# Taking the maximum of the value weights in four pieces, one per feed-forward step

## What is computed

```
x = x + 0.5 * ffn(layernorm(x))
x = x + attn(layernorm(x))
x = x + 0.5 * ffn(layernorm(x))

ffn:  h = x
      for blk in range(3):                    # three blocks
          y = qlora_linear(h, 2*blk)          # dequantised 128x128 weight, bias, low-rank term
          y = gelu(layernorm(y, g[blk], b[blk]))
          h = h + qlora_linear(y, 2*blk+1)
attn: xq, xk = x Q[h], x K[h]                 # 16 heads, rank 64
      attn = softmax(xq xk^T / sqrt(128))
      out  = sum over heads of attn x VO[h]   # VO: 16 x 128 x 128
```

## Time and profile before

| | |
|---|---|
| median of 3 runs | 987.42 us |
| profiled execution, its own time | 987.76 us |
| its span | 986.0 us |
| TensorE busy | 956.5 us (97%) |
| VectorE busy | 855.1 us (87%) |
| ScalarE busy | 807.4 us (82%) |
| GpSimd busy | 829.5 us (84%) |
| granted TensorE clock, mean | 0.997 |

### The profile page before, as it was taken

The page is one execution under the profiler, slowest core; times in us unless marked ns, Lnnn a source line. Parts: engine busy times, 40 slices in busy tenths (PEclk is TensorE's granted clock), DMA queues, the critical chain, the costliest instruction groups (busy, mean ns, idle before and its releaser), DMA issues.

```text
span 986.0 us, 19436 instructions
## 1 busy us (share of the span) xinstructions
PE 956.5 (97%) x6005; PEld 509.7 (52%) x6005; DVE 855.1 (87%) x1741; ACT 807.4 (82%) x1341; POOL 829.5 (84%) x938
## 2 busy tenths in 40 slices
PE   4889899999999999999999999999999999999998
PEld 4668344444444444444444444444444444444777
DVE  7678999999999999999999999999999988986664
ACT  4866788888888888888888888888888988888774
POOL 3645699899998999899999999999999998899552
PEclk9999999999999999999999999999999999999999
DMA  9000322222222222222222222222222222221002
GB/s 253 1 1 9 89 65 65 65 59 68 61 59 62 63 63 59 62 63 65 66 65 65 65 65 65 65 65 57 63 62 61 64 61 61 63 62 33 2 1 86
DMA packets 71744, 59.89 MB, mean 61 GB/s; under 512 B 11168, under 2 KB 70560, under 8 KB 71648
## 3 DMA queue, kind: packets, MB, share of 16 engines
q1 hardware_dynamic: 71392, 58.31, 24.0%
q10 hardware_dynamic: 256, 0.39, 0.2%
HBM read 6.23 MB, written 2.10 MB: 8 GB/s over the span
## 4 chain that ended last, share of the span: by engine, by line
PE 91%; DVE 5%; POOL 2%; issue 1%; DMA 1%; ACT 0%; SPq 0%; POOLq 0%; DVEq 0%; ACTq 0%
PE ps L1219 12%; PE ps L1211 11%; PE ps L1221 11%; PE ps L1220 11%; PE ps L1212 11%; PE ps L1204 7%; PE ps L1195 3%; PE ps L1238 3%; PE ps L1234 3%; PE ps L1235 3%; PE ps L1113 3%; PE ps L1196 3%; PE ps L1197 3%; PE ps L1142 2%; PE ps L1123 1%; PE ps L1154 1%
## 5 line engine op out<-in xcount | busy, mean ns | idle before, releaser
L470 POOL TENSOR_TENSOR p_lo<-work_b,p_hi 128x1024 f16<-128x1024 f32 x256 | 540.1, 2131 | 46.3 <-ACT p_hi L615 45.7
L920 DVE TENSOR_REDUCE mcol<-ps 128x2 f16<-128x1024 f32 x256 | 301.4, 1222 | 2.2 <-PE ps L1204 2.1
L610 ACT ACTIVATE work_b<-ps,exp_scale 128x1024 f32<-128x1024 f32 x256 | 271.5, 1111 | 36.5 <-PE ps L1212 36.3
L615 ACT ACTIVATE p_hi<-work_b 128x1024 f16<-128x1024 f32 x256 | 256.0, 1055 | 0.0
L1211 PE MATMUL ps<-head_ops 128*128 128x512 f16 x512 | 194.1, 379 | 2.9 <-DVE mcol L920 1.5
L1219 PE MATMUL ps<-p_hi,xn_hi 128*128 128x512 f16 x512 | 194.7, 380 | 0.9 <-POOL p_lo L470 0.9
L1220 PE MATMUL ps<-p_hi,xn_lo 128*128 128x512 f16 x512 | 194.0, 379 | 0.0
L1221 PE MATMUL ps<-p_lo,xn_hi 128*128 128x512 f16 x512 | 194.0, 379 | 0.0
L1212 PE MATMUL ps<-head_ops 128*128 128x512 f16 x512 | 194.0, 379 | 0.0
L479 POOL TENSOR_TENSOR x<-x,o_sb 128x512 f32<-128x512 f32 x126 | 160.2, 1271 | 5.4 <-POOL rstd L447 0.2
L931 DVE STREAM_TRANSPOSE head_ops<-mcol 32x128 f16<-32x128 f16 x512 | 155.4, 304 | 9.3
(11 more groups left out here) (139 smaller groups left out, 1378.9 us busy)
## 6 DMA issues: line engine op xcount, KB each, us to landing
head_ops<-pair_ops SPq DMA_DIRECT2D x512, 64.0 KB, 2.0
head_ops<-pair_ops SPq DMA_DIRECT2D x128, 128.0 KB, 2.4
x<-x_dram SPq DMA_DIRECT2D x8, 256.0 KB, 5.9
out<-x SPq DMA_DIRECT2D x8, 256.0 KB, 2.5
vo_last<-wvo_dram SPq DMA_DIRECT2D x1, 1024.0 KB, 11.9
qk<-wq_dram SPq DMA_DIRECT2D x1, 512.0 KB, 5.2
qk<-wk_dram SPq DMA_DIRECT2D x1, 512.0 KB, 6.0
scl<-scales_dram ACTq DMA_DIRECT2D x8, 48.0 KB, 5.3
```

The costliest lines, as they stand in the source:

```text
L470: pool.tensor_tensor(p_lo[:, k % 2, rows, :], p32[:, k % 2, rows, :], p_hi[:, k % 2, rows, :], ALU.subtract).then_inc(plo_done, 1)
L610: nc.scalar.activation(p32[:, k % 2, 2 * a:2 * a + 2, :], s_ps[a], ACT.Exp, scale=exp_scale[:, 0:1]).then_inc(exp_done, 1)
L615: nc.scalar.activation(p_hi[:, k % 2, 2 * a:2 * a + 2, :], p32[:, k % 2, 2 * a:2 * a + 2, :], ACT.Copy).then_inc(phi_done, 1)
L920: nc.vector.tensor_reduce(mcol[:, pair % 2, :, t, 0], max_ps[pair == 1][t % 2], AX.X, ALU.max, negate=True).then_inc(max_red, 1)
```

## The change

The reduce over the 2048 columns of the value weights is cut into four reduces of 512 columns (four heads). Their results go to a new tile `vo_amax` of four columns, and a fifth, small reduce takes the maximum of these four. Piece q waits for 2(q+1) folds where the one reduce waited for 8. The pieces are issued in steps 3, 3, 4 and 5 and the maxima of Q and K in steps 1 and 2 where they were in steps 2 and 3. Also the place within the step is another one: K's maximum and the first, third and fourth piece stand between `seed` and `z_scaled`, Q's maximum and the second piece behind `z_scaled`.

```
+        vo_amax = sb("vo_amax", [128, 4])
...
-                dve.wait_ge(vo_folded, H // 2)
-                link(dve, nc.vector.tensor_reduce(amax[:, 2:3], vo32[:, :, :].rearrange("p h d -> p (h d)"), AX.X,
-                                                  ALU.max, apply_absolute_value=True))
-                nc.vector.tensor_scalar(amax[:, 0:3], amax[:, 0:3], 1e-30, None, ALU.max).then_inc(prep_v, 1)
+                q = n - 2
+                heads = slice(q * H // 4, (q + 1) * H // 4)
+                dve.wait_ge(vo_folded, 2 * (q + 1))
+                link(dve, nc.vector.tensor_reduce(vo_amax[:, q:q + 1], vo32[:, heads, :].rearrange("p h d -> p (h d)"),
+                                                  AX.X, ALU.max, apply_absolute_value=True))
+                if q == 3:
+                    link(dve, nc.vector.tensor_reduce(amax[:, 2:3], vo_amax[:, :], AX.X, ALU.max))
+                    nc.vector.tensor_scalar(amax[:, 0:3], amax[:, 0:3], 1e-30, None, ALU.max).then_inc(prep_v, 1)
...
                 seed(0, i)
+                if i == 2:
+                    weight_maxima(1)
+                if i == 3:
+                    weight_maxima(2)
+                if i in (4, 5):
+                    weight_maxima(i)
                 if i >= 1:
                     z_scaled(0, i - 1)
-                if i in (2, 3):
-                    weight_maxima(i - 2)
-                if i == 5:
-                    weight_maxima(2)
+                if i == 1:
+                    weight_maxima(0)
+                if i == 3:
+                    weight_maxima(3)
```

## The result

| | before | after |
|---|---|---|
| median of the runs | 987.42 us (7 runs, 986.00 to 987.95) | 983.17 us (7 runs, 983.11 to 984.57) |
| profiled execution, its own time | 987.76 us | 983.50 us |
| its span | 986.0 us | 981.7 us |

The ratio is 0.9964 with a 95% interval of 0.9953 to 0.9975: the change makes the kernel 4.25 us faster by the medians, 4.3 us by the two spans.

A forecast was written before the change was run, and what follows sets the result against it. TensorE, busy 97% of the span, was taken to bound the kernel. 3.03 us (start of `turn_tops`) + 1.58 us + 0.11 us (clock) = 4.7 us, giving 982.7 us (76%), range 981.6 to 985.1 us.

The forecast's parts named there:

- The place: TensorE's 2.62 us wait for the clamp ahead of `turn_tops`, said to cost twice: by idle time and by slow clock.
- The clock term: Behind the wait the clock stays at 2.4 GHz: `lin2(3)` takes 1.58 us less and `turn_z(4)` 0.11 us less.
- The rival that doubted this term: The clock falls all the same, or did not fall in the median run: 3.0 us remain, 984.4 us; 10%.
- The start of `turn_tops`: `turn_tops` starts at about 52.55 instead of 55.58 us, released by `z_scaled(4)`: 3.03 us.
- The last piece: Between `seed(5)` and `z_scaled(4)`, with small reduce and clamp: 1.13 us, ending at 51.4 to 52.0 us.
- The hidden edits: Q's and K's maxima and the other pieces, in earlier steps: VectorE works 0.7 us more in all, none on the path.
- The rival by which the reduces hold GpSimd up: The six reduces delay `newton(4)` by 5.1 us, so `turn_tops` starts at 57.6 us: 989.5 us; 3%.
- the move of Q's and K's maxima: Q's maximum ahead of `seed(2)` lets `step_h(0)` begin about 1.1 us earlier; TensorE gains 0.4 to 0.6 us.
- the first two rivals: Clock gain not won: 984.4 us, 10%; last piece ends late, `turn_tops` moves by 2.1 us: 983.6 us, 6%.
- the case that gives it back: Waits at the beginning of attention grow or the clock falls there, losing most or all: 986 to 987.4 us; 5%.
- the wait of 0.41 us: TensorE's wait for `step_h(0)` at 40.96 us; its removal was to end `lin1(6)` near 52.4 us.

The follow-up runs named there:

- Run 9: Kernel before, with two matmuls of 512 columns that nobody reads put into TensorE's wait ahead of `turn_tops`: 986.14 us.
- run 10: Kernel before, unchanged, profiled once more to see its clock: that execution took 985.99 us.
- run 11: Kernel before, unchanged, profiled another time to see its clock: that execution took 986.36 us.
- run 12: Kernel before, unchanged, profiled a further time to see its clock: that execution took 986.11 us.
- run 4: Changed kernel without its four pieces; the small reduce reads four columns of Q's weights instead: 982.99 us.
- Run 7: Changed kernel with the reduce of each of the four pieces issued a second time: 984.25 us.
- run 2: Changed kernel with the maxima of Q and K left in steps 2 and 3 behind `z_scaled`: 984.31 us.
- run 1: Kernel before, with Q's and K's maxima moved a step earlier and the whole uncut reduce with its clamp put ahead of `z_scaled(4)`: 984.22 us.
- run 3: Changed kernel with all four pieces behind `z_scaled` in steps 2 to 5: 984.58 us.
- run 5: Kernel before, its reduce in the old place over only the first 1024 columns of the value weights: 985.31 us.
- run 6: Kernel before, its reduce in the old place over only 512 columns of the value weights: 984.63 us.
- run 8: Changed kernel with a Gelu of a single column added at the head of ScalarE's program to load its table early: 983.93 us.

## Why the prediction was right

**The place.** That TensorE's wait for the clamp was the only thing the change could win, and that it was paid twice, held. The two parts (2.60 + 1.69 us) make up the 4.3 us by which the spans differ.

**The clock term** was forecast at 1.58 + 0.11 = 1.69 us and measured at 1.69 us between the two profiles. Run 9 shows that it follows from the idle stretch: with the wait kept and filled, the time falls to 986.14 us and the upper group disappears. The rival that doubted this term was half right, though. By the groups the slow stretch comes in some 6 of 10 executions, and the median of the kernel before lies in the group that has it (987.42 us is near its lower edge). Had one more of the seven runs fallen into the lower group, its median would have been near 986.2 us and the gain about 3.0 us, that of the rival. By the shares of the groups (24 and 34 of 58) this happens to about one set of seven runs in three, an estimate, where the rival had 10%. So that the gain came out as 4.25 us and not as 3.0 us was in part luck; the 983.17 us of the changed kernel owe nothing to it. Against the two groups the gain is 2.9 and 4.6 us. The changed kernel has no such second group from this place: none of its seven runs shows a mean clock under 0.998.

**The start of `turn_tops`** was forecast at 52.55 us and came at 52.98 us; this term was mis-sized, 3.03 against 2.60 us. The step that failed is that TensorE would be through `lin1(6)` near 52.4 us and that `z_scaled(4)` would then set the time. In the profiled execution `lin2(0)` started at 38.46 us where it had started at 37.69 us before. From there TensorE worked through without a gap of note, so it was the path itself. The reason lies ahead of the change's place: the slow stretch of the first units fell later (30.3 to 33.8 us instead of 28.5 to 31.9 us) and slowed other matmuls. Executions of the unchanged kernel differ by as much. Runs 10, 11 and 12 start `lin2(0)` at 37.14, 38.62 and 38.24 us, and in the last two, whose slow stretch fell late too, TensorE doesn't wait for `step_h(0)` at all:

```profile
38.62 1.98 PE L1142 MATMUL ps<-work_a,wt 128*128 128x512 f32 x4 [0.23 <-ACT work_a L551]
41.36 0.39 PE L1110 MATMUL ps<-bias_rows,ones_b 128*128 128x512 bf16 x1
```

So the 0.4 to 0.6 us that I had taken for the end of this wait are there to be had in some executions only, and I had read them from a single one. In run 4, where `lin2(0)` started at 37.21 us, it went as I had forecast: TensorE was early, `z_scaled(4)` released it, and `turn_tops` started at 52.33 us. That kernel lacks the pieces, but they cost little (0.2 to 0.3 us), so a part of the 0.43 us is this execution and not the change. How much of it remains in the median (983.17 against 982.7 us) stays open: runs at 983.11 us weren't profiled.

**The last piece** with the small reduce and the clamp was expected to end at 51.4 to 52.0 us and ended at 52.14 us, because `seed(5)` ended at 51.15 us where I had 50.3 to 50.9 us. `newton(4)` ended at 52.06 us, so it just fitted. The 0.68 us for 512 columns was met exactly, the 0.18 us of the small reduce came as 0.16 us. Run 7 shows that the fit is tight: each piece taken twice costs 1.1 us.

**The hidden edits** were hidden. Run 4 prices all four pieces together at 0.2 to 0.3 us. The rival by which the reduces hold GpSimd up is out: with the reduces beside them GpSimd's small operations took 0.20 to 0.23 us, like this one beside the last piece.

```profile
51.29 0.20 POOL L403 TENSOR_TENSOR u_u<-u_t,u_var 128x8 f32<-128x8 f32 x1
```

**What I had too small**, by run 2, is the move of Q's and K's maxima. I gave it 0.4 to 0.6 us as a by-product that brings TensorE forward. Run 2 comes out 1.1 us slower than the changed kernel, and two waits come back and not one. How much of the 1.1 us they make in an execution with the slow stretch near 30 us isn't shown.

**The chances** don't add up as written. The forecast and the first two rivals (76, 10 and 6%) make 92% and not 91%, and the case that gives it back has 5%, where 6% was put within 0.2% of no change.

## What to carry to other kernels

A wait of the bounding engine is priced by its own length and by what it does to the speed behind it; filling the wait with work that nobody reads (run 9) separates the two. A reduce that isn't on the path is best cut so that each piece fits into the time for which its engine waits anyway, and put ahead of the operation that this wait belongs to; by the medians the move brought three quarters of the gain here and the cut the rest. A row taken from one profile holds for one execution: the wait of 0.41 us on which a term of the forecast rested is missing from two of three further profiles. A kernel whose times lie in two groups should be compared group by group, since the median of a few runs can jump by their distance.

## What the runs showed of the hardware

Behind an idle stretch of 2.62 us TensorE's granted clock fell to 1.2 GHz in one profiled execution of the kernel before (0.52 from 55.7 to 59.2 us). In three others, with idle stretches of 2.50 to 2.62 us at the same place, it stayed at 2.4 GHz (1.00). So a single profile doesn't tell whether such a stretch costs the clock; the two groups of the timed runs, 24 and 34 of 58, say that it often does. Behind the idle stretches of 0.43 to 1.44 us at this place (runs 1 and 3 to 7, one profile each) and that of 0.79 us in run 9 no profile shows a fall.

The slow stretch near 30 us goes with another idle stretch, the one of TensorE ahead of the transposes of the first layer norm (L1077 in the kernel before), which differs between executions. In eight of the fourteen profiles it is 3.58 to 3.64 us, in two (the changed kernel and run 11) 2.15 to 2.16 us, and all ten have the slow stretch. In the four others (runs 2, 8, 9 and 10) it is 1.74 to 1.86 us, and the clock stays full. No run changed this idle stretch alone, so that it is the cause isn't shown.
